# Rows times the Gram matrix in two halves of 64 rows and 64 columns

## What is computed

```python
x = layer_norm(dense_t @ Wd.T, gd, bd)
y = layer_norm(jnp.einsum('bnd,ed->bne', sparse_t, Ws), gs, bs)   # 26 rows of each sample
y = jnp.einsum('bne,pn->bep', y, Wsi)
y = layer_norm(y, gsi, bsi)
T = jnp.concatenate([x[:, None, :], swapaxes(y, 1, 2)], axis=1)   # 33 rows of 128
Z = jnp.einsum('bnd,bmd->bnm', T, T)
out = layer_norm(Z[:, TRIL_I, TRIL_J] @ Wl.T, gl, bl) * mask
h = relu(concat([out, dense]) @ W_top1 + b_top1)
y = relu(h @ W_top2 + b_top2) @ W_top3
```

## Time and profile before

| what | value |
|---|---|
| time, median of 3 runs | 632.09 us (631.2 to 634.22) |
| the profiled execution's own time | 628.93 us |
| its span, first to last instruction | 627.1 us |
| TensorE busy (products / loads) | 580.9 us (93%) / 438.0 us (70%) |
| VectorE, ScalarE, GpSimd busy | 409.2, 317.6, 396.8 us |
| mean granted TensorE clock | 0.984 |

### The profile page before, as it was taken

One profiled execution on the slowest core, in us unless ns is written; L12 is line 12 of the kernel. 1 busy time (PEld: TensorE's weight loads), 2 busy tenths in 40 slices (PEclk: granted clock), 3 DMA queues, 4 the chain that ended last, 5 costly groups with the idle time before them and its releaser, 6 DMA issues.

```text
span 627.1 us, 18003 instructions
## 1 busy us (share of the span) xinstructions
PE 580.9 (93%) x7035; PEld 438.0 (70%) x7035; DVE 409.2 (65%) x789; ACT 317.6 (51%) x711; POOL 396.8 (63%) x420
## 2 busy tenths in 40 slices
PE   0699899999999999999999999999999999999865
PEld 0565667677877777777777777777777777777554
DVE  3757877676766667676766677676766767676501
ACT  0135455656465555646455555656455555646321
POOL 3677767776777777677777776767676776720000
PEclk9979799999999999999999999999999999999989
DMA  8511331515151522515151421515151421503030
GB/s 273 167 27 45 69 64 46 88 36 85 45 86 35 82 48 45 85 36 87 44 86 36 74 56 40 87 33 86 41 87 34 74 56 39 87 22 54 20 45 2
DMA packets 95845, 39.96 MB, mean 64 GB/s; under 512 B 75985, under 2 KB 87633, under 8 KB 95697
## 3 DMA queue, kind: packets, MB, share of 16 engines
q1 hardware_dynamic: 82514, 26.05, 21.4%
q0 software_dynamic: 13312, 13.66, 11.4%
HBM read 30.75 MB, written 8.92 MB: 63 GB/s over the span
## 4 chain that ended last, share of the span: by engine, by line
PE 80%; ACT 7%; DMA 5%; DVE 5%; issue 2%; POOL 1%; SPq 0%; ACTq 0%; DVEq 0%
PE p_y L522 18%; PE p_u L473 10%; PE p_q L484 8%; PE p_z L543 7%; PE p_b L569 6%; PE p_b L576 6%; PE p_b L586 5%; PE p_b L597 3%; PE p_u L470 3%; DMA rows<-in_table,index 3%; ACT zc L630 3%; PE p_b L599 3%; PE p_b L602 3%; PE p_t L451 3%; PE p_a L512 1%
## 5 line engine op out<-in xcount | busy, mean ns | idle before, releaser
L417 POOL DMA_INDIRECT rows<-in_table,index x416 | 396.6, 953 | 157.5 <-issue 115.2
L522 PE MATMUL p_y<-ut,wy 65*128 65x512 f32 x256 | 126.3, 616 | 0.1
L646 ACT COPY ut<-p_u 64x512 f32<-64x512 f32 x128 | 74.3, 580 | 57.7 <-PE p_u L473 56.2
L855 DVE TENSOR_REDUCE y_sum<-y_sq 128x32 f32<-128x1024 f32 x64 | 78.1, 1220 | 30.1 <-ACT y_sq L683 29.3
L827 DVE TENSOR_TENSOR prod<-p_q,rows 128x512 f32<-128x512 f32 (+1 forms) x64 | 37.8, 590 | 82.0 <-PE p_q L484 82.0
L473 PE MATMUL p_u<-wsi_c,rows_n 128*128 128x192 f32 (+4 forms) x512 | 89.7, 320 | 0.0
L473 PEld LDWEIGHTS p_u<-wsi_c,rows_n 128*128 128x128 f32 x512 | 77.9, 194 | 16.0 <-issue 16.0
L868 DVE TENSOR_TENSOR feat<-p_y,y_rs 128x1024 f32<-128x1024 f32 x64 | 78.4, 1224 | 7.2
L683 ACT ACTIVATE y_sq<-p_y 128x1024 f32<-128x1024 f32 x64 | 65.6, 1025 | 24.4 <-PE p_y L522 23.7
L543 PEld LDWEIGHTS p_z<-feat 128*32 128x32 f32 x4096 | 45.6, 109 | 42.8 <-issue 36.6
L484 PE MATMUL p_q<-gram,et 128*128 128x128 f32 x416 | 62.3, 290 | 8.3 <-ACT et L637 8.3
(11 more groups left out here) (108 smaller groups left out, 756.0 us busy)
## 6 DMA issues: line engine op xcount, KB each, us to landing
products<-zs SPq DMA_DIRECT2D x64, 136.0 KB, 1.8
zb<-products SPq DMA_DIRECT2D x64, 136.0 KB
rows<-in_table,index POOLq DMA_INDIRECT x416, 2.4
dense_x<-in_dense SPq DMA_DIRECT2D x16, 128.0 KB
wl<-in_Wl_rows SPq DMA_DIRECT2D x1, 1280.0 KB, 12.1
wsi<-in_Wsi_blocks SPq DMA_DIRECT2D x1, 1248.0 KB, 5.4
w<-in_W SPq DMA_DIRECT2D x2, 512.0 KB
masks<-in_masks SPq DMA_DIRECT2D x1, 960.0 KB, 7.6
```

Of the source, the lines that this page charges most:

```text
L417: pool.indirect_dma_start(out=rows[:, j, g, :], out_offset=None, in_=a["table"], in_offset=bass.IndirectOffsetOnAxis(ap=index[:, n, t, g % ...
L522: last = nc.tensor.matmul(p_y[:, 512 * h:512 * h + 512], wy[:], ut[:, 4 * h:4 * h + 4, :].rearrange("d g c -> d (g c)"), start=True, stop= ...
L646: nc.scalar.copy(ut[0:D, GU // 2 * h:GU // 2 * (h + 1), :].rearrange("d g c -> d (g c)"), p_u[D * h:D * h + D, :]).then_inc(ut_ready, 1)
L855: nc.vector.tensor_reduce(y_sum[:], y_sq[:], AX, ALU.add).then_inc(y_summed, 1)
```

## The change

`gram` becomes 128 x 64: C once on partitions 0 to 63 and once on 64 to 127. Each pair has two matrix products in the place of one: half h takes partitions 64h to 64h+63 of `et[:, m, :]` (64 x 128) as the stationary operand and the same partitions of `gram` (64 x 64) as the moving one. The products of the first halves go to `p_q`, those of the second to `p_t`, which are now two neighbouring banks of one PSUM tensor `p_qt`. Since `p_t` is in use longer, the transposes of a unit wait for `q_used` of the unit before (in the place of `et_ready`), and the products themselves no longer wait for it. VectorE's product L827 reads both banks through patterns of one dimension more.

```diff
-        gram = sb("gram", [128, 128])
+        gram = sb("gram", [128, D])
...
-        p_t, p_q, p_u, p_z, p_a, p_b = (pb(n) for n in ("p_t", "p_q", "p_u", "p_z", "p_a", "p_b"))
+        p_u, p_z, p_a, p_b = (pb(n) for n in ("p_u", "p_z", "p_a", "p_b"))
+        p_qt = ctx.enter_context(nc.psum_tensor("p_qt", [128, 2, 512], F32))
+        p_q, p_t = p_qt[:, 0, :], p_qt[:, 1, :]
...
-                        after(pe, et_ready, k)
+                        after(pe, q_used, k)
                         for m in range(PAIRS[j]):
                             last = nc.tensor.transpose(
                                 p_t[:, 128 * m:128 * m + 128],
...
                         pe.wait_ge(et_ready, k + 1)
-                        after(pe, q_used, k)
                         for m in range(PAIRS[j]):
-                            last = nc.tensor.matmul(p_q[:, 128 * m:128 * m + 128], et[:, m, :], gram[:],
-                                                    start=True, stop=True)
+                            for h in range(2):
+                                last = nc.tensor.matmul(p_qt[:, h, D * m:D * m + D], et[D * h:D * h + D, m, :],
+                                                        gram[D * h:D * h + D, :], start=True, stop=True)
                         last.then_inc(q_done, 1)
...
-                nc.vector.tensor_scalar(gram[D * h:D * h + D, D * h:D * h + D], p_q[D * h:D * h + D, 0:D], 1.0 / E,
+                nc.vector.tensor_scalar(gram[D * h:D * h + D, :], p_q[D * h:D * h + D, 0:D], 1.0 / E,
                                         None, ALU.mult).then_inc(prepared, 1)
...
-                        nc.vector.tensor_tensor(prod[:, 0:m].rearrange("r g d -> r (g d)"), p_q[:, 0:D * m],
-                                                rows[:, j, 0:m, :].rearrange("r g d -> r (g d)"), ALU.mult).then_inc(q_used, 1)
+                        nc.vector.tensor_tensor(prod[:, 0:m].rearrange("r (t h) d -> r h t d", h=2),
+                                                p_qt[:, :, 0:D * PAIRS[j]].rearrange("r h (t d) -> r h t d", d=D),
+                                                rows[:, j, 0:m, :].rearrange("r (t h) d -> r h t d", h=2), ALU.mult
+                                                ).then_inc(q_used, 1)
```

## The result

The changed kernel takes 646.23 us in the median of 4 runs (645.42 to 647.85), the kernel before 633.15 in the median of 4: a ratio of 1.0219 with a 95% interval of 1.0164 to 1.0273. Slower was right, 639.3 was too little by 7 us, and the range of 628 to 648 held the time.

A forecast was written before the change was run, and what follows sets the result against it. TensorE's own list was taken as the bound. Fourteen turns at +0.49 us gave +6.9, the first eight units +0.3: +7.2 us on 628.93 made 636.1 profiled, 639.3 us against the 632.09 median; range 628 to 648.

The forecast's parts named there:

- the turn: One loop turn of four steps, 35.5 us before: +0.49 us, in fourteen turns +6.9 us.
- the first eight units: Units ahead of the loop, behind gathers and ScalarE at a clock of 0.91: between 0 and 1 us, taken as +0.3.
- rival (b): Changed block: halves staggered, second group begins one load late, +0.107 x 56 = +6, 645 us; chance 0.08.
- What bounds the kernel: Steady state: TensorE's own list is on the path, busy 492.4 of 500 us; the rest is cover.
- Loads set the pace, row groups load side by side: Changed block: loads at about 0.107 us each pace it; halves load together, 0.214 us a pair against 0.221 before.
- (a): Changed block: row groups load one after another, each pair 0.214 us more, about 681 us; chance 0.12.
- (d): Changed block: half-height loads take half the time, a pair costs 0.107 us, 623 us in all; chance 0.04.
- Two changes of shape: Entering and leaving the block: each loses 0.095 us emptying the array, and the next load is no longer hidden.
- (c): Block's ends: no change of shape to pay between 128 and 64 partitions, -3.4 us in 14 turns, 628.7; chance 0.10.
- Steps 0, 1 and 3: The block in three of a turn's four steps, j = 0, 1 and 3: +0.27, +0.05 and -0.07 us.
- Step 2: The block in step j = 2: both emptyings and an exposed transpose load are paid, +0.24 us.
- new wait (e): VectorE's L827 reads two banks so slowly that transposes wait beyond 3.9 us of cover; 0.02 together with a lower clock.

The follow-up runs named there:

- full-height kernel: Changed kernel with both 64-column products per pair over all 128 partitions, noughts filling gram; 1096.18 us against 1056.77 and 1094.08 against 1073.87 for the kernel before.
- edit of the noughts: Kernel before, with the noughts' product ahead of the mixing over 128 partitions instead of one; ratios 0.982, 0.974 and 0.977, and 998.98 us against 1064.95.

## Why the prediction was right, and where it was short

The forecast of 639.3 us was 6.9 short. Of that, 1.1 is the kernel before, whose median is now 633.15; 1.5 is the turn (14 x 0.11); and 4.4 are the first eight units (4.7 - 0.3). That the range held the time is in part luck: its upper end stood for rival (b), which is out, and not for what moved the time.

- **What bounds the kernel.** Right. Nothing but TensorE's list got longer, and the total followed.
- **Loads set the pace, row groups load side by side.** Right: 0.22 us a pair, starts 7 ns apart; 0.45 where both halves take the full height; no gain from half the columns. So (a), (b) and (d) are out: the loads of the two halves alternate from the first on, and a load of 64 partitions takes as long as one of 128.
- **Two changes of shape.** Right in mechanism and size, so (c) is out. The Trainium skill, TensorEngine Tiling (Array Packing), Key Properties, says that a change of mode drains the engine and a change of tile does not. The trace agrees: 0.17 us without a load ahead of the block, none between the halves. The Trainium skill, TensorEngine Tiling (Array Packing), Theoretical Speedup, gives up to 2x for a dimension of 64 or less. This is not met here: the matrix product for a pair is split in two, and each half's load of 128 columns costs what the whole load did.
- **Steps 0, 1 and 3** came within 0.02 us, over 13 turns within 0.03. **Step 2** was set at +0.24, which is what p_y shows (+0.25), and measured +0.15 up to p_z. Before, p_y's second half waited there for ScalarE's copy (1.98 from start to end, 1.88 after). The later start takes that wait away; I had used this cover in step 1 and overlooked it in step 2.
- **A turn** was set at +0.49 and is +0.60. The block gives 0.45 to 0.47. The rest is in the pairwise products, at which the prediction put nothing; their busy time from 105 to 590 us, before and then after:

```profile
105.00:590.00 485.00, 47.15 (x3548) 39.29 (x3552) 1.00 0.33 59
```
```profile
105.00:590.00 485.00, 48.02 (x3456) 39.37 (x3456) 1.00 0.33 58
```

  At 64 records a unit that is 0.850 us a unit before and 0.889 after, 0.16 a turn. By single starts the added time lies in step 0: from first to last start 0.59 us in the mean before and 0.75 after, where a pause of 0.2 stands ahead of the last record or the one before it in 12 of 13 turns (0.57 in the kernel with halves ahead of the loop only). Such pauses came in the other steps before, too. The full-height kernel has as many instructions and no such pause in step 0 wherever it does not stand (18 of 26 turns), so their number alone is not the cause. It could still be their supply, since its block lasts 0.7 us longer; that is not shown.
- **The first eight units.** This is the term that was mis-sized: +0.3, between 0 and 1. The trace of the changed kernel has +12.1 there, that with halves ahead of the loop only +9.0, and by medians it is 13.1 - 14 x 0.60 = 4.7 and 7.1. Three things were wrong in the step. I took the clock of 0.91 from the earlier trace rows as that of these units, but it counts the time ahead of the first rise as full. I priced the units at the full clock, while unit 1 ran at half: from its transposes to L552 it takes 38.31-29.89 = 8.42 us before and (L554) 39.86-30.85 = 9.01 after, +0.59. Of this 0.20 lies in the transposes, which before began at the full clock; the other 0.39 stands against +0.05 in my sum for such a step. And I took the time at the lower clock as given: I had put a lower clock and the new wait together at 0.02. Between the two traces units 4 to 7 lose 10.7 of the 12.1 us, with 37.5 us at the lower level against 6.8, so there it is most of the loss. How much of the 4.7 us by medians it is stays open: three of the changed kernel's four runs have a mean clock of 0.979, the same as the mean over the eleven runs of before beside the kernel with halves ahead of the loop only, and the line through those runs can't be trusted to divide it.
- **The new wait (e)** showed up once, 0.85 us at unit 6 of the kernel with halves ahead of the loop; before, TensorE stood 0.86 us at the same place for a gather. It decides nothing.

What stays open is why the clock came back late. In both kernels with halves in turn 1 it stayed low over that turn's blocks and came back with the last layer's long products, at 98.9 and 100.5 us; in the kernel before in unit 6. It is open too why the short first rise at 26.7 us is missing in both. Other runs of before had as low a mean clock (0.965), so part of it may be chance that the changed kernel only makes likelier.

## What to carry to other kernels

Before a matrix product is split over row groups, ask which of its two records sets its pace. Where the stationary operand has as many columns as the moving one or more, it is the load, and halving rows and moving columns halves nothing of it. Price each entry to and exit from a smaller shape from the gaps that the trace has already, here 0.1 us of emptying and a load in the open, and check at each whether a wait covers it; gaps that are there already, such as a one-partition product of noughts between full ones, are the first to remove. And price the start of a kernel apart: where the engine's clock has not settled, a small cost goes with more time at the lower level, which in these traces cost more than the change itself. A mean clock is read with its first record beside it.

## What was not expected of the hardware

On five chips single runs of the kernel before took 1020 to 1093 us, elsewhere 627 to 638. The waits of the full-height kernel on one of them:

```profile
ACT zs L690 <- remote: 280.1, 41, 11.3
...
PEld p_z L545 <- issue: 147.6, 200, 2.0
```

Engines stand up to 11 us for nothing that the profile of this core shows, and TensorE's loads stand 200 times amid bursts of short products, 0.7 us in the mean. The edit of the noughts, worth 0.28 us a step and so 1.7% over 64 steps, brought 1.8 to 6% there; what the rest comes from is not known.
